# Fused adaLN block: prologue with another order of means and modulation parts, and squares summed by TensorE alone

## The reference

```python
mod = silu(c) @ wmod                      # c: (2, 1024), wmod: (1024, 6*1024)
sa, ca, ga, sb, cb, gb = mod              # each (2, 1, 1024)
ga = sign(ga) * max(|ga|, 0.25); gb likewise
h = layernorm(x) * (1 + ca) + sa          # x: (2, 2048, 1024)
# attention over the batch: for each of the 1024 features, a 2 x 2 softmax
# of the products of the two batch rows over all 2048 tokens
x = x + ga * (h + prob @ h)
h = layernorm(x) * (1 + cb) + sb
x = x + gb * ((silu(h @ Wg.T) * (h @ Wu.T)) @ Wd.T)    # F = 2752
```

## Time and profile before

| | us |
|---|---|
| median of 3 runs | 2721.07 (2720.78 to 2721.39) |
| profiled execution | 2726.44, span 2724.6 |
| TensorE busy in the span | 2624.9 (96%) |
| VectorE busy | 1799.1 (66%) |
| ACT busy | 1306.6 (48%) |
| GpSimd busy | 181.2 (7%) |
| start of the first product | 217.06 |

### The profile page before, as it was taken

How to read it: one execution, slowest core, us unless ns; L and a number is a source line. 1 busy time by engine, 2 the same in 40 slices (tenths; PEclk the granted TensorE clock), 3 DMA queues, 4 the chain that set the end, 5 groups by cost and what they waited for, 6 DMA issues and landing times. The chain is left out here.

```text
span 2724.6 us, 33611 instructions
## 1 busy us (share of the span) xinstructions
PE 2624.9 (96%) x11968; PEld 2127.0 (78%) x11968; DVE 1799.1 (66%) x2507; ACT 1306.6 (48%) x2058; POOL 181.2 (7%) x225
## 2 busy tenths in 40 slices
PE   6468999999999999999999999999999999999999
PEld 3236888887888888888887888888888888888887
DVE  7979777867677767677757666657555555555544
ACT  4566456555456655466555333334433433343332
POOL 6500011000011000011000000000000000000000
PEclk8779999999999999999999999999999999999999
DMA  8675566648666558665658877779567658557655
GB/s 337 249 297 165 196 219 221 198 155 284 197 223 202 186 166 300 197 217 188 207 155 307 268 242 254 254 259 319 214 229 274 211 205 290 212 207 268 236 196 172
DMA packets 291285, 625.35 MB, mean 230 GB/s; under 512 B 22192, under 2 KB 91824, under 8 KB 285232
## 3 DMA queue, kind: packets, MB, share of 16 engines
q1 hardware_dynamic: 272400, 550.85, 59.2%
q0 software_dynamic: 17088, 59.78, 6.6%
q10 hardware_dynamic: 1632, 12.58, 1.1%
HBM read 437.79 MB, written 185.34 MB: 229 GB/s over the span
## 5 line engine op out<-in xcount | busy, mean ns | idle before, releaser
L1731 PE MATMUL ps<-x_hi_P,w_hi 128*128 128x512 f32 x2416 | 942.7, 390 | 15.6 <-DVE x_lo_P L1215 9.1
L1732 PE MATMUL ps<-x_lo_P,w_hi 128*128 128x512 f32 x2416 | 941.3, 390 | 0.0
L1733 PE MATMUL ps<-x_hi_P,w_lo_P 128*128 128x512 f32 x2416 | 940.9, 389 | 0.0
L766 ACT CAST w_hi<-w_raw_P 128x512 fp32r<-128x512 f32 x604 | 374.6, 622 | 435.3 <-PE ps L1733 419.5
L1198 DVE TENSOR_TENSOR w_lo_P<-w_raw_P,w_hi 128x512 fp32r<-128x512 f32 x604 | 413.2, 685 | 206.0 <-PE ps L1733 184.4
L1731 PEld LDWEIGHTS ps<-x_hi_P,w_hi 128*128 128x128 f32 x2416 | 454.1, 188 | 113.7 <-issue 12.8
L1733 PEld LDWEIGHTS ps<-x_hi_P,w_lo_P 128*128 128x128 f32 x2416 | 454.1, 188 | 94.8
L1732 PEld LDWEIGHTS ps<-x_lo_P,w_hi 128*128 128x128 f32 x2416 | 454.3, 188 | 93.1
L1798 PE MATMUL ps<-hh,w_hi 128*128 128x512 f32 x1232 | 479.4, 389 | 0.5 <-DVE hb L1395 0.5
L1799 PE MATMUL ps<-hl,w_hi 128*128 128x512 f32 x1232 | 479.3, 389 | 0.0
L1800 PE MATMUL ps<-hh,w_lo 128*128 128x512 f32 x1232 | 479.2, 389 | 0.0
(11 more groups left out here) (189 smaller groups left out, 2038.7 us busy)
## 6 DMA issues: line engine op xcount, KB each, us to landing
w_raw_P<-wgu SPq DMA_DIRECT2D x294, 256.0 KB, 3.0
w_raw_P<-wsum_dram SPq DMA_DIRECT2D x252, 256.0 KB, 3.8
hl_raw<-h_dram SPq DMA_DIRECT2D x84, 768.0 KB, 7.5
w_raw<-wds_dram SPq DMA_DIRECT2D x64, 704.0 KB, 4.7
h_dram<-hb SPq DMA_DIRECT2D x33, 1280.0 KB, 5.6
w_raw<-wdn SPq DMA_DIRECT2D x48, 704.0 KB, 5.0
wsum_dram<-w_raw_P SPq DMA_DIRECT2D x84, 256.0 KB, 3.0
x_raw_P<-xr_dram SPq DMA_DIRECT2D x21, 1024.0 KB, 12.0
```

The costliest lines, as they stand in the source:

```text
L766: s.copy(w_hi[m % HI_RING][:], w_raw[(name, u)][:]).then_inc(whi_ready, 1)
L1731: mm(to, hi[:, w], xh, start=fresh and k == 0, stop=False, skip_group_check=not fresh)
L1732: mm(to, hi[:, w], xl, start=False, stop=False, skip_group_check=not fresh)
L1733: ins = mm(to, lo[:, w], xh, start=False, stop=k == KH - 1, skip_group_check=not fresh)
```

## The change

The changed kernel does eight things. (1) The first chunk is loaded in two halves of 1 MB with a semaphore each (`x_half` for tiles 0 to 3). TensorE sums the first half itself; DVE adds the four tiles of the second (`sum_half`). (2) Of the other chunks of round 0, POOL adds four tiles of each (`sum_tiles`), also of (1,1), which DVE did. (3) In round 1 nothing is added ahead: TensorE sums all eight tiles; the means of pair 1 go into the banks 6 and 7 (`ps_mean_late`), so they need only the normalising of round 0's pair 0 to be done. (4) `add_squares` and `sq_pair` are gone; TensorE takes both tiles of each square. (5) In both rounds the means and modulation parts are in another order on TensorE, and DVE inverts (0,0) before it centres (1,1). (6) In the finish, TensorE does `mean_f(0)` behind two parts of group 2 instead of six, with the other four in front of `variance_f(0)`. (7) DVE does two tiles of `sum_f(1)` before `centre_f(0)`, and `scale_f(0)` before `centre_f(1)`; `scale_f(1)` comes behind the operands of the first product. ACT does all of `scaled_f` before it squares, and the `w_hi` casts behind x_hi of P1. (8) The last two modulation parts come behind the first two products.

```diff
+PRESUM = 4
-                    sp.dma_start(tok(xbuf[a % 2][:, h]), x[chunk + h].rearrange("p (k t) -> p k t", k=KD)).then_inc(
-                        x_loaded[a % 2][h], 16)
+                    first = KH if a == h == 0 else 0
+                    to, of = tok(xbuf[a % 2][:, h]), x[chunk + h].rearrange("p (k t) -> p k t", k=KD)
+                    if first:
+                        sp.dma_start(to[:, 0:first], of[:, 0:first]).then_inc(x_half, 16)
+                    sp.dma_start(to[:, first:KD], of[:, first:KD]).then_inc(x_loaded[a % 2][h], 16)
...
-                if t == 0:
-                    sum_tiles(0, 1)
-                    add_squares(0, 0, range(1))
-                    sum_tiles(1, 0)
-                    add_squares(0, 0, range(1, NSQ))
...
+            sum_tiles(0, 1)
+            sum_tiles(1, 0)
+            sum_tiles(1, 1)
...
             scaled_f(0, range(KD))
-            scaled_f(1, range(KH))
-            squares_f(0, range(2))
-            scaled_f(1, range(KH, KD))
+            scaled_f(1, range(KD))
             s.activation(eps_root, eps_t, ACT.Sqrt)
-            squares_f(0, range(2, NSQ))
+            squares_f(0, range(NSQ))
             root_f(0)
             copy_rows(2)
-            w_hi_cast(0)
-            w_hi_cast(1)
-            squares_f(1, range(NSQ))
-            root_f(1)
             act.wait_ge(xh_stored[0], 64)
             for k in range(KH):
                 modulate_f(0, k)
+            squares_f(1, range(NSQ))
+            root_f(1)
             act.wait_ge(rawf_ready, KH)
             s.copy(x_hi["P1"][:], raw_b11[:]).then_inc(xhi_ready, 1)
+            w_hi_cast(0)
+            w_hi_cast(1)
...
                 if t == 0:
-                    sum_tiles(0, 0)
+                    sum_half()
                 centre(0, 0)
                 centre(0, 1)
-                if t == 0:
-                    sum_tiles(1, 1)
                 centre(1, 0)
+                invert(0, 0)
                 centre(1, 1)
-                invert(0, 0)
                 invert(0, 1)
...
-            sum_f(0)
+            sum_f(0, 0, KD)
+            sum_f(1, 0, 2)
             centre_f(0)
-            sum_f(1)
+            sum_f(1, 2, 6)
             invert_f(0)
-            centre_f(1)
+            sum_f(1, 6, KD)
             take(3, ps_mod[1], ROWS[2], half, half + 2)
             link(v.tensor_scalar(cb1[:], mod[:, half + 1], 1.0, None, ALU.add))
             v.nop().then_inc(mods_taken, 1)
-            dve.wait_ge(df_ready, 2 * NSQ)
             scale_f(0)
-            invert_f(1)
-            scale_f(1)
+            centre_f(1)
             for u in range(2):
                 w_sums_123(0, u)
+            invert_f(1)
             w_lo_part(0)
             w_lo_part(1)
             x_lo_f("P1", raw_b11)
+            dve.wait_ge(df_ready, 2 * NSQ)
+            scale_f(1)
...
+                    bank, ks = ps_mean_late[h] if t and u else ps_mean[u][h], range(KD) if t else range(PRESUM, KD) if i else range(KH)
...
                     for j in range(NSQ):
-                        pe.wait_ge(sq_added, t * (4 * NSQ) + (i * NSQ + j + 3))
-                        for b in range(NTB):
-                            ins = mm(ps_mean[u][h][b * QP:(b + 1) * QP, 0:P], ones[:, 0:QP], sq_pair[:, j % 2, b * P:(b + 1) * P],
-                                     start=j == 0, stop=j == NSQ - 1)
-                        ins.then_inc(sq_pair_used, 1)
+                        pe.wait_ge(sq_ready, t * (4 * NSQ) + (i * NSQ + j + 1))
+                        for k in range(SQ_PER):
+                            for b in range(NTB):
+                                ins = mm(ps_mean[u][h][b * QP:(b + 1) * QP, 0:P], ones[:, 0:QP], sq[:, j % 2, k, b * P:(b + 1) * P],
+                                         start=j == k == 0, stop=j == NSQ - 1 and k == SQ_PER - 1)
+                        ins.then_inc(sq_used, 1)
...
+                else:
+                    means(1, 0)
+                    means(1, 1)
+                    parts(0, range(3, GROUP[0]))
                     variances(0, 0)
                     variances(0, 1)
                     spread(0, 0)
                     spread(0, 1)
+                    parts(1, range(2))
                     variances(1, 0)
...
-            parts(2, range(6))
+            parts(2, range(2, 4))
...
+            mean_f(0, range(KD))
+            parts(2, range(4, GROUP[2]))
             variance_f(0)
-            parts(2, range(7, GROUP[2]))
-            mean_f(1)
+            mean_f(1, range(4))
             spread_f(0)
             turn(2, ps_mod[1], ROWS[2], 0)
+            mean_f(1, range(4, 6))
+            mean_f(1, range(6, KD))
...
+                if m == 2:
+                    parts(3, range(2, GROUP[3]))
```

146 lines of the change are left out of this document (58 added, 88 removed).

## The result

| | before | after |
|---|---|---|
| median, us | 2721.0 | 2701.69 (2700.33 to 2705.58) |
| ratio | | 0.9928 (95%: 0.9912 to 0.9943) |
| profiled execution, span | 2726.44, 2724.6 | 2705.58, 2703.8 |
| coefficients ready (end of `coef`) | 150.1 | 138.7 |
| first product starts | 217.06 | 186.87 |

The change takes 19.3 off (19.6 by the ratio, 15.5 to 23.9 by its interval). Faster was right, the size was not.

The account below looks back on a forecast made before the run. The start of P6 bounds it, everything behind shifts: 2.8 at `take` plus 10.0 in the finish make 12.8, less 1.4 for P6 at half clock, so 11.4 less: 2709.7 us, range 2703 to 2717.5.

Parts of the forecast that it names:

- Round 0: VectorE's normalising in round 0 starts at 40.0 instead of 44.62 and ends at 72.1, 11.2 earlier.
- the lock's price of 0.47 a sum: Round 0's 16 sums of products cost 1159 ns beside GpSimd, 683 with it idle; 7.6 us leave VectorE.
- the end of the waits for the means: Finish: VectorE's two waits for means, 8.6 and 5.0, both go through the new order.
- the first product: TensorE's first product starts at 195.6 instead of 217.06; VectorE can't follow up most of that advance.
- The finish term of 10.0: From the coefficients to P6: 10.0 us less, so P6 starts 77.9 behind them.
- the waits in front of x_lo P5: Finish: VectorE waits 3.2 for ACT's late `modulate_f(1)`, held by `copy_rows(3)` and parts 22 and 23.
- Round 1, start: here most of it is given back: TensorE's 64-pass block, 58.5 to 88.1, then three parts to 91.3, delay variance (0,0); normalising starts at 105.0 instead of 109.00.
- I take 4.4 in all: Round 1's normalising: stalls at root (1,0), 2.4 to 4.9, and second inverse, 0 to 1.4, taken as 4.4.
- the cooled P6: TensorE may fall to half clock before P6, costing up to 2.8 over 14 matmuls; half, 1.4, was taken.
- a second round starting before 100: Sign against the forecast: round 1 starting before 100 would mean the 64 passes are not what bounds it.
- the new waits that the prediction names: Finish: VectorE waits 0.9 for chunk 0's root, 0.4 for w_hi casts, 3.2 for `modulate_f(1)`.
- larger gain: Rival, chance 0.22: full clock in round 1, `take` at 138.0, no cooling before P6; 15.3 less, 2706.

Follow-up runs that it names:

- a_round1: Changed kernel, round 1 reordered on TensorE: variance (0,0) before the last 16 passes of the block, parts 3 to 8 singly between squares; 2694.64 us, ratio 0.9899.
- b_squares: Kernel before with one edit: TensorE sums the squares alone, 16 passes a square; 2712.01 us, ratio 0.9964.
- after_again: The changed kernel unaltered, measured again; 2699.32 us, ratio 0.9916.
- b_squares_finish: Kernel before with two edits: squares summed by TensorE alone, and the changed kernel's order from the coefficients on; 2707.75 us, ratio 0.9945.
- a_whole: Changed kernel with the first chunk loaded in one piece again; 2702.41 us, ratio 0.9925.
- a_parts_first: Changed kernel with modulation parts 22 and 23 in front of the first product instead of behind the two P1; 2702.92 us, ratio 0.9923.
- a_pairs: Changed kernel with GpSimd's pair sums of the squares put back, 8 passes a square; 2708.88 us, ratio 0.9950.
- a_lock: Changed kernel with 24 idle GpSimd additions in a buffer of their own; 2705.16 us, ratio 0.9934.
- b_finish: Kernel before with one edit: the changed kernel's order from the coefficients on (VectorE, ACT, TensorE); 2714.13 us, ratio 0.9970.

## Why the prediction was wrong

**Right.** The bound (the start of P6, everything behind it a shift). Round 0: 40.0, 72.1 forecast, 39.26, 70.23 measured; the lock's price of 0.47 a sum; the end of the waits for the means; the first product (195.6 less the 8.6 that came earlier makes 187.0, measured 186.87); P6 77.9 behind the coefficients, measured 76.3. The finish term of 10.0 measures 9.1 over all profiles, and 8.2 alone, 3.5 or 6.8 taken back in the timed runs. Of the waits in front of x_lo P5, 3.2 forecast, 2.29 measured, part is luck: in seven of ten profiles it is 0.6 to 0.7.

**Wrong, the failed step: "Round 1, start: here most of it is given back".** The mechanism is as forecast: the block of 64 passes and the parts behind it hold variance (0,0), `invert(0,0)` waits behind it (9 forecast, 6.30), centring (1,1) stands behind that, and a_round1 shows that this sets the time. Round 0 ends 7.2 earlier than in b_squares, whose coefficients come at the same time, and round 1's normalising starts only 2.1 earlier: 5.1 is given back there. Its size was off in each of its parts, always to the same side:

- The block starts at 55.20, not 58.5: 0.7 from an earlier round 0, 1.0 from a stall of VectorE at `invert(1,0)` that did not come because variance (1,0) ran at full clock, and 1.6 for which the prediction had no working at all.
- It lasts 27.7, not 29.6. Of these 1.9, 0.8 is the half clock that I had put on its first five passes. The other 1.1 is a misreading of the earlier trace rows: eight passes last 3.60, but the next group starts 3.43 behind their start (rows below). The pace is 0.43 a pass; 3.60 by 8, which is 0.45, spreads the tail of the last pass over all of them.
- The parts take 2.6, not 3.2. All three were taken at full clock; it is the same slip, a part of 1.07 alone is 0.87 in a row of three.
- The root is ready 4.9 behind them, not 5.2, and the way from there to normalising is 0.1 shorter.

Together 6.2: normalising at 98.81, not 105.0. The rows of before behind the second point, eight passes and what follows them:

```profile
16.21 3.60 PE L1588 MATMUL ps<-xbuf,ones 128*128 128x512 f32 x8
19.64 1.02 PE L1593 MATMUL ps<-presum,ones 128*128 128x512 f32 x2
```

The 0.8 of half clock was a fair term that this one profile didn't have. In after_again the block starts 0.7 earlier, at half clock, and ends at the same time:

```profile
54.46 28.52 PE L1564 MATMUL ps<-xbuf,ones 128*128 128x512 f32 x64
```

**Wrong, the term beside it: "I take 4.4 in all" of stalls in round 1.** One stall of 1.98 came, the second did not: 2.4. With the 6.2 that is the 8.6 at the coefficients. The finish adds 1.6, the cooled P6 takes 1.6 to 2.2 where I had 1.4: 9.4 more than forecast in the span, 7.9 in the median.

**A sign that was set wrong.** The prediction said that a second round starting before 100 would mean that the 64 passes don't bound it. It started at 98.81, and they do. The sign took the block's forecast end for certain; the row that tells is the wait of `invert(0,0)`, which came.

**Sums and a reading that don't close.** 87.9 less the waits of 13.7 and 2.2 is 72.0, not 71.6, and the new waits that the prediction names (0.9, 0.4, 3.2) make 4.5, not the 5.6 of its check. The 1.1 between them is about the wait for the turn, which the prediction doesn't name and which was 1.2 in the profile after; the measured waits are 4.2. And the first mean's half clock is read from its length: the granted clock of the earlier trace rows is 1.00 from 10 to 20 us, while the passes up to 15 stand 0.85 apart, so that column doesn't show the first passes.

**The price of it.** About half of the 8.6 was TensorE at half or at full clock (0.8, 1.0 and the 2.4), where I took half or a middle and the profile had full; 1.7 was the pace misread, and 1.6 had no working. The prediction had written the faster side down as a rival, larger gain, but at 2706, with only the stalls and the turns in it and the block as forecast. A bound for the block itself (64 times 0.43 from 55) was never worked out, and the range had no room for it.

**What it was not.** I first took the gain beyond the forecast to be a gift of more passes. Twice the passes in the old kernel raised the granted clock and gained nothing. What the change gains up to the coefficients, the squares alone give too: 6 of b_squares' 11.3 are collisions of GpSimd with VectorE that went (1.0, 2.7 and 2.3), 2.2 its profile's clock. The new rounds take more away in round 0 and give it back at the start of round 1 (5.1) and in its stall (1.98); what they are worth, some 5, shows mostly behind the coefficients.

**Open.** Why the spread and the part at 51.4 ran at full clock in one of six profiles and partly at half in the other five; with the same instructions up to there, the coefficients scatter by 3.4 (135.43 to 138.83). Which piece of the new rounds, the tile sums or the order of means and parts, gives the 5 between b_squares_finish and a_whole was not tried alone.

## What to carry to other kernels

When a resource is taken out of a chain, follow the gain to the next engine that bounds the stage and give that engine's work a lower and an upper price from rows; a block whose start and pace both hang on the clock needs both ends in the range. Take the pace of a block from the starts of two neighbouring groups, not from the length of a short group divided by its count. Take the length of a stage that hangs on weights and on the clock from more than one profile, since one was 4 off here. A passage in which an engine waits in turn for another (here between two squares) is the place for independent work, and a long block in front of a chain is worth cutting where the first piece of the chain is ready.

## What the runs showed of the hardware

- A group of GpSimd additions whose two inputs are the same SBUF buffer, in memory that no one else uses, made VectorE's two-input sum of products 1024 instead of 688 ns, though nobody waited for it.
- TensorE's clock in short passages differs from run to run. In six profiles of kernels that are the same up to there, the last spread of round 0 took 1.13, 1.34, 1.62, 1.84 or 2.05, the part behind it 1.07 to 1.94, and the one profile with both at full clock had its coefficients 3.1 to 3.4 earlier.
- Behind gaps of about the same length TensorE ran at either clock. Behind 2.01 to 2.10 of idle time P5 was at half clock from its first matmul in four profiles (a_parts_first, after_again, a_pairs, a_round1); in two (a_lock, b_finish) the first six matmuls ran at full clock and the next ones, 0.43 apart, at half. P6 began at full clock behind 2.02 (0.47, 0.39) and then fell in the profile after, and did not fall at all behind 1.79 and 1.81 (b_finish, a_lock). Behind 3.34, P5 was at half clock from its first matmul in all three profiles (after, a_whole, b_squares_finish). The Trainium skill's page TensorE: Matmul & The Clock Gate, section What's actually happening, has the throttled state as the default that activity releases. The rows agree in that idle time stands before each of these falls, but not every gap brought one.
